# Softmax reciprocals of an attention layer's first two blocks computed in 16 columns, with three SyncE transfers to fold and spread them

## The reference, cut to what matters

```python
attn = jnp.einsum('bhdi,bhdj->bhij', q * scale, k)
attn = attn + pos[..., :, None] + pos[..., None, :]
attn = jax.nn.softmax(attn, axis=-1)
y = jnp.einsum('bhij,bhdj->bhdi', attn, v)
```

## Time and profile before

| | us |
|---|---|
| median of 3 runs | 514.74 (514.13 to 515.56) |
| profiled execution, its own time | 514.55 |
| its span in the profile | 512.8 |
| outside the span | 1.75 |
| mean granted TensorE clock | 0.98 |

### The profile page before, as it was taken

The page is one execution under the profiler, slowest core; times in us unless marked ns, Lnnn a source line. Parts: engine busy times, 40 slices in busy tenths (PEclk is TensorE's granted clock), DMA queues, the critical chain, the costliest instruction groups (busy, mean ns, idle before and its releaser), DMA issues.

```text
span 512.8 us, 7031 instructions
## 1 busy us (share of the span) xinstructions
PE 479.3 (93%) x2268; PEld 238.7 (47%) x2268; DVE 360.1 (70%) x687; ACT 273.3 (53%) x522; POOL 217.8 (42%) x203
## 2 busy tenths in 40 slices
PE   8799999999989899999999999999999989998996
PEld 6454444443237565444444322664544444432463
DVE  7599888976164568987887823738988787832573
ACT  3138776767514324876766762131777765764032
POOL 8300021001000002898879991000699888896000
PEclk9969999999998998999999999998999999999999
DMA  5330432000000054487944440034457854442002
GB/s 145 56 57 20 137 65 34 1 2 2 1 0 1 15 123 104 82 203 159 207 89 84 83 79 5 1 88 109 92 120 154 182 105 83 84 83 42 1 0 82
DMA packets 16419, 38.18 MB, mean 74 GB/s; under 512 B 4870, under 2 KB 6030, under 8 KB 16256
## 3 DMA queue, kind: packets, MB, share of 16 engines
q1 hardware_dynamic: 11088, 21.72, 17.7%
q0 software_dynamic: 5152, 16.00, 16.9%
q10 hardware_dynamic: 144, 0.02, 0.0%
HBM read 4.76 MB, written 1.05 MB: 11 GB/s over the span
## 4 chain that ended last, share of the span: by engine, by line
PE 68%; DVE 15%; DMA 4%; ACT 4%; issue 3%; SPq 3%; POOL 2%; ACTq 0%; POOLq 0%; DVEq 0%
PE PV L927 15%; PE S L889 15%; PE S L916 11%; DVE max L662 10%; PE S L1037 4%; DMA k_stack<-kL 4%; PE M L943 3%; PE PV L844 2%; PE S L870 2%; DVE rec_sb L692 2%; PE M L870 2%; PE PV L870 2%; PE S L907 2%; PE S L1082 2%; PE PV L863 1%
## 5 line engine op out<-in xcount | busy, mean ns | idle before, releaser
L662 DVE TENSOR_REDUCE max<-S 128x1 f32<-128x512 f32 x384 | 239.8, 669 | 20.8 <-PE S L889 20.6
L514 ACT ACTIVATE E<-S 128x512 f32<-128x512 f32 x384 | 212.6, 601 | 76.2 <-PE S L916 72.2
L450 POOL TENSOR_TENSOR SUMS<-E 128x512 f32<-128x512 f32 x126 | 167.0, 1476 | 123.9 <-ACT E L514 123.8
L889 PE MATMUL S<-k_stack,q_stack 126*128 126x512 f32 x384 | 183.2, 490 | 13.5 <-DVE max L662 8.7
L916 PE MATMUL S<-q_stack,k_stack 128*128 128x512 f32 x384 | 154.6, 411 | 2.7 <-ACT E L514 1.5
L889 PEld LDWEIGHTS S<-k_stack,q_stack 126*128 126x128 f32 x384 | 74.4, 194 | 92.9 <-DVE max L662 64.7
L927 PE MATMUL PV<-E,V 128*32 128x512 f32 x768 | 95.4, 599 | 1.7 <-ACT pv_sb L521 1.7
L916 PEld LDWEIGHTS S<-q_stack,k_stack 128*128 128x128 f32 x384 | 72.6, 191 | 33.3 <-ACT E L514 20.6
L692 DVE RECIPROCAL rec_sb<-den_sb 128x64 f32<-128x64 f32 (+1 forms) x54 | 35.7, 665 | 35.0 <-ACT den_sb L531 35.0
L503 ACT ACTIVATE mHL<-S 4x128 fp32r<-4x128 f32 x48 | 12.6, 263 | 55.2 <-PE S L907 55.2
L927 PEld LDWEIGHTS PV<-E,V 128*32 128x32 f32 x768 | 20.0, 109 | 45.2 <-issue 28.3
(11 more groups left out here) (180 smaller groups left out, 335.5 us busy)
## 6 DMA issues: line engine op xcount, KB each, us to landing
SUMS<-SUMS POOLq DMA_DIRECT2D x30, 512.0 KB, 5.1
k_stack<-kH SPq DMA_DIRECT2D x32, 128.0 KB, 3.0
q_stack<-qH SPq DMA_DIRECT2D x40, 64.0 KB, 2.0
k_stack<-kL SPq DMA_DIRECT2D x16, 128.0 KB, 3.2
q_stack<-qH SPq DMA_DIRECT2D x16, 128.0 KB, 2.3
q_stack<-mHL SPq DMA_DIRECT2D x96, 2.0 KB
q_stack<-qL SPq DMA_DIRECT2D x20, 64.0 KB, 2.0
X<-x_in_dram SPq DMA_DIRECT2D x2, 512.0 KB, 5.5
```

Of the source, the lines that this page charges most:

```text
L450: pool.tensor_tensor(SUMS[:, slot, :], E[:, E_PLAN[s][0], :], E[:, E_PLAN[s + 1][0], :], ALU.add).then_inc(sum_ready, 1)
L514: act.activation(E[:, slot, :], B[:, ring_of_scores(s) % B_RING, :], ACT.Exp, scale=1.0 if l == 0 else float(HEAD_DIM[l]) ** -0.5).then_in ...
L662: dve.tensor_reduce(max8[:, m % 2, r:r + 1], A[:, n % A_RING, :], AX.X, ALU.max, negate=True).then_inc(a_used, 1)
L889: pe.matmul(A[:, n % A_RING, :], q_stack[0:SHIFT_ROW, slot, q0:q0 + P], k_stack[0:SHIFT_ROW, slot, k0:k0 + HALF], start=True, stop=True).t ...
```

## The change

In each layer the reciprocals of blocks 0 and 1 are computed on four rows' worth of numbers instead of 128 rows, since the 32 rows of a head hold the same number. SP issues three transfers a block. `fold_sums` takes one row a head (four rows of 512) and lays it out as 128 partitions of 16 columns (`den_in`), 128 pieces of 64 bytes. DVE makes one reciprocal of 128x16 (`folded_reciprocals`, s = 66 and s = 98). `reciprocal_rows` writes the result back as rows 0, 32, 64, 96 of `den_sb`. `spread_reciprocals` copies each of these four rows to its head's 32 rows of `rec_sb`, 256 KB in pieces of 2 KB. On SP's list `fold_sums` of block 0 stands behind the last head's load (ahead of the weight load in layer 1), `reciprocal_rows` behind shift row 9, `spread_reciprocals` behind shift row 10; for block 1 the three stand behind shift rows 12, 13 and 14. POOL's `normalise` waits for the spread.

In layer 0 the fold reads `pv_sb`, and the gather matmul on PE and the copy to `den_sb` on ACT remain only for the later blocks. In layers 1 and 2 the fold reads `den_sb`, and ACT's copy moves from s = 59, 91, 123 to s = 54, 86, 118. The rest of the layer is as before. The diff, without the declarations of four semaphores and a removed constant:

```diff
@@ -42,8 +42,9 @@
...
-REC_PARTS = (8, 8, 2, 2)
-REC_STEP = 64
+FOLDED = 2
+REC_STEP = 66
+PER_ROW = HALF // DP
@@ -128,6 +129,8 @@
...
+        den_in = sb("den_in", [P, PER_ROW])
+        rec_out = sb("rec_out", [P, PER_ROW])
@@ -264,10 +267,15 @@
...
+        REC_L = 2 * (BLOCKS - FOLDED)
+        PV_OUTS = (4, 3, 3)
+        DEN_OUTS = (BLOCKS - 1 - FOLDED, BLOCKS - 1, BLOCKS - 1)
...
-            return REC_L * l + sum(REC_PARTS[:b + 1])
-
-        PV_OUTS, DEN_OUTS = (4, 3, 3), 3
+            return REC_L * l + 2 * (b - FOLDED + 1)
+        def den_count(l, b):
+            return sum(DEN_OUTS[:l]) + b + 1 - (0 if l else FOLDED)
@@ -320,6 +328,30 @@
...
                                  mHL[:, m % 2, r, :].bitcast(F32)).then_inc(shift_dma[m % 2], 16)
+            def fold_sums(l, b):
+                if l == 0:
+                    sp.wait_ge(pv_out, pv_count(l, b))
+                    src, row = pv_sb, DP // 2
+                else:
+                    sp.wait_ge(den_out, den_count(l, b))
+                    src, row = den_sb, 0
+                sp.dma_start(den_in[:, :], src[row:P:DP, :].rearrange("u (d n) -> u d n", n=PER_ROW)).then_inc(dens_folded, 16)
+            def reciprocal_rows(l, b):
+                sp.wait_ge(recs_folded, FOLDED * l + b + 1)
+                sp.dma_start(den_sb[0:P:DP, :].rearrange("u (d n) -> u d n", n=PER_ROW), rec_out[:, :]).then_inc(recs_rows, 16)
+            def spread_reciprocals(l, b):
+                sp.wait_ge(recs_rows, 16 * (FOLDED * l + b + 1))
+                sp.wait_ge(att_ready, (BLOCKS - 1) * l + b)
+                sp.wait_ge(att_tail, 2 * l)
+                sp.dma_start(rec_sb[:, :],
+                             den_sb[0:P:DP, :].rearrange("u (o n) -> u o n", o=1)
+                             .to_broadcast([HEADS_B, DP, HALF])).then_inc(recs_spread, 16)
@@ -360,11 +392,18 @@
...
                         shift_rows(l, h + 1)
+                fold_sums(l, 0)
                 if l == 1:
...
                     shift_rows(l, j)
+                    if j in (9, 13):
+                        reciprocal_rows(l, (j - 9) // HEADS_B)
+                    if j in (10, 14):
+                        spread_reciprocals(l, (j - 10) // HEADS_B)
+                    if j == 12:
+                        fold_sums(l, 1)
             for n in range(4):
@@ -421,7 +460,10 @@
...
                 g, f = b // 2, b % 2
-                pool.wait_ge(rec_ready, rec_count(l, b))
+                if b < FOLDED:
+                    pool.wait_ge(recs_spread, 16 * (FOLDED * l + b + 1))
+                else:
+                    pool.wait_ge(rec_ready, rec_count(l, b))
                 pool.tensor_tensor(att[:, g, HALF * f:HALF * (f + 1)], pv_sb[:, :], rec_sb[:, :],
@@ -523,11 +565,11 @@
...
                 if l == 0:
-                    act.wait_ge(gathered, b + 1)
+                    act.wait_ge(gathered, b - FOLDED + 1)
                 else:
                     act.wait_ge(den_done, DENS_L * (l - 1) + 2 * (b + 1))
-                if l + b:
-                    act.wait_ge(rec_ready, rec_count(l, b - 1) if b else REC_L * l)
+                act.wait_ge(recs_spread, 16 * (FOLDED * l + min(b, FOLDED)))
+                act.wait_ge(rec_ready, REC_L * l)
                 act.activation(den_sb[:, :], M[:, :], ACT.Copy).then_inc(den_out, 1)
@@ -564,9 +606,10 @@
...
                         numerators_out(l, (s - 57) // 32)
-                    den_step = 59 if l else 62
-                    if s >= den_step and (s - den_step) % 32 == 0:
-                        denominators_out(l, (s - den_step) // 32)
+                    den_step = 54 if l else 62
+                    b = (s - den_step) // 32
+                    if s >= den_step and (s - den_step) % 32 == 0 and (l or b >= FOLDED):
+                        denominators_out(l, b)
                 if l == 0:
@@ -675,20 +718,24 @@
...
+            def folded_reciprocals(l, b):
+                n = FOLDED * l + b
+                dve.wait_ge(dens_folded, 16 * (n + 1))
+                dve.wait_ge(recs_rows, 16 * n)
+                dve.reciprocal(rec_out[:, :], den_in[:, :]).then_inc(recs_folded, 1)
             def reciprocals(l, b, part):
-                wide = HALF // REC_PARTS[b]
-                cs = slice(wide * part, wide * (part + 1))
+                cs = slice(QUARTER * part, QUARTER * (part + 1))
                 if part == 0:
...
                     if b < BLOCKS - 1:
-                        dve.wait_ge(den_out, DEN_OUTS * l + b + 1)
+                        dve.wait_ge(den_out, den_count(l, b))
                     elif l == 0:
-                        dve.wait_ge(gathered, BLOCKS)
+                        dve.wait_ge(gathered, BLOCKS - FOLDED)
                     else:
                         dve.wait_ge(den_done, DENS_L * l)
-                    if b == 0 and l:
-                        dve.wait_ge(att_tail, 2 * l)
                 dve.reciprocal(rec_sb[:, cs], den_sb[:, cs] if b < BLOCKS - 1 else M[:, cs]).then_inc(rec_ready, 1)
@@ -697,7 +744,7 @@
...
-                    dve.wait_ge(rec_ready, REC_L * l + sum(REC_PARTS[:-1]) + part + 1)
+                    dve.wait_ge(rec_ready, rec_count(l, BLOCKS - 2) + part + 1)
@@ -738,11 +785,10 @@
...
                         split(l, LATE_DVE[l][s])
-                    b, part = (s - REC_STEP) // 32, (s - REC_STEP) % 32 // 2
-                    if 0 <= b < 2 and s % 2 == 0 and part < REC_PARTS[b]:
-                        reciprocals(l, b, part)
-                for part in range(REC_PARTS[2]):
-                    reciprocals(l, 2, part)
+                    if s >= REC_STEP and (s - REC_STEP) % 32 == 0 and (s - REC_STEP) // 32 < FOLDED:
+                        folded_reciprocals(l, (s - REC_STEP) // 32)
+                for part in range(2):
+                    reciprocals(l, BLOCKS - 2, part)
                 last_block(l)
@@ -932,7 +978,7 @@
...
                 if k == 0 and b:
-                    pe.wait_ge(den_out, DEN_OUTS * l + b)
+                    pe.wait_ge(den_out, den_count(l, b - 1))
                 first = HEADS_B * b
@@ -952,8 +998,8 @@
...
                 pe.wait_ge(pv_out, b + 1)
-                if b:
-                    pe.wait_ge(den_out, b)
+                if b > FOLDED:
+                    pe.wait_ge(den_out, b - FOLDED)
                 pe.matmul(M[:, :], gather[:, :], pv_sb[:, :], start=True, stop=True).then_inc(gathered, 1)
@@ -1008,8 +1054,8 @@
...
                             denominators(l, BLOCKS - 1, 0)
-                    if l == 0 and s >= 60 and (s - 60) % 32 == 0:
-                        gather_sums((s - 60) // 32)
+                    if l == 0 and s == 60 + 32 * FOLDED:
+                        gather_sums(FOLDED)
                 for t in range(5, TILES):
```

More of the change, by code:

```diff
@@ L195, in attention_chain @@
         rec_ready, att_ready, att_tail = sem("rec_ready"), sem("att_ready"), sem("att_tail")
+        dens_folded, recs_folded, recs_rows, recs_spread = (sem("dens_folded"), sem("recs_folded"), sem("recs_rows"),
+                                                            sem("recs_spread"))
         out_done, x_ready = sem("out_done"), sem("x_ready")
@@ L252, in sum_count @@
             return (l - 1) * SUMS_L + min(PAIRS * j + k + 1, SUMS_L)
-        REC_L = sum(REC_PARTS)
         RING_L = STEPS + UNITS_L
```

## The result

The changed kernel takes 510.87 us (median of 5 runs, 508.97 to 512.11) against 515.28 for the kernel before in the same comparison, a ratio of 0.9918 with a 95% interval from 0.9896 to 0.9941. Seven more runs gave a median of 510.49 us, ratio 0.9913 (0.9878 to 0.9949). The forecast was 508.5 in a range of 506.9 to 512.0: the direction and the range hold, but 4.4 us came where 6.2 were worked out.

The account below looks back on a forecast made before the run. Layer 0 was taken as bound by PE with DVE in the way, the ends of layers 1 and 2 by POOL and transfers. 514.55 - 4.07 - 2.2 = 508.3 us profiled, 508.5 for the median; range 506.9 to 512.0.

Parts of the forecast that it names:

- Layer 0: Two of three gather matmuls and the stalls of sixteen reciprocal parts go: 4.07 us summed over the layer's periods.
- base period: Undisturbed period between L927 groups in layer 1, 271.70 to 278.14: 6.44 us, against which longer periods were compared.
- last period with maxima: Layer 0, 115.69 to 122.01, only six maxima left: gain taken as 0.40 us, between 0 and 0.81.
- relief in layers 1 and 2: Shorter periods put PE 1.6 us ahead in a layer; 1.1 us a layer taken (0.8 to 1.6), 2.2 for both.
- period with the head's load: Layer 1, up to 256.49: PE stands for the load with or without reciprocals; gain 0, at most 0.4 us.
- 6.6 to 8 fits into 8.9: Block 1 of layer 1: the 256 KB spread takes 6.6 to 8 us, within 8.9 us before POOL wants it.
- rival A: Spread lands at about 10 us, holding POOL's normalise of block 1 by 1.1 us in layers 1 and 2: 510.5 us; chance 0.12.
- ScalarE's copy: Denominators' copy five steps earlier: at s = 118 it delays PE by one copy, within the 0.4 us PE can spare.
- The last 0.4 comes after that and is lost: End of layers 1 and 2: PE's last 0.4 us of gain comes after POOL's idle time and is lost to POOL.
- C: Fold lands late, 7.6 us instead of 5.59; DVE holds PE 2 us in layers 1 and 2: 512.3 us; chance 0.06.
- D: DVE isn't what lengthens the periods; only the two gather matmuls are won, 1.62 us: 512.9 us; chance 0.06.
- B: Spread takes 13 us, 4.1 late; layers 1 and 2 each lose 3.0 us: 516.5 us, slower; chance 0.06.

Follow-up runs that it names:

- both edits: Changed kernel with the spread's source rows in partitions 0, 36, 72, 108 and ScalarE's copy of the denominators back at s = 59, 91, 123: 507.62 us, ratio 0.9862.

## Why the prediction was right and where it was not

**Layer 0.** Each term came out: 4.07 predicted, 4.02 measured. The gathers were shown alone (1.6), the stalls alone (2.4), and they add. The base period from layer 1 was the right one for layer 0. The last period with maxima, taken by analogy at 0.40 between 0 and 0.81, was 0.41.

**The relief in layers 1 and 2.** 0.80, 0, 0.40 and 0.40 were predicted, and the groups in the first trace give 0.80, 0, 0.39 and 0.42. That the period with the head's load gives nothing was right in that trace; in the second it was 0.6 shorter (7.12 us), but it was also short, 7.26, with the reciprocals back, so this is not their relief.

**The spread.** The step that failed is "6.6 to 8 fits into 8.9". The window was 8.4 us (294.22, when POOL was ready, less 285.84), and the transfer took 9.6. Without the sums' folds the higher estimate, 6.6, was near the 7.1 measured; what was mis-sized is the term for the load beside it, 2.5 us and not up to 1.4. That the folds are this load is argued from layer 0, which has none; no run took them away. It isn't a fixed price either: from one port the same place added only 0.2 to 0.5 us (12.1 to 12.3 and 12.6). What followed is rival A, with its mechanism, its place and the length of its hold: 1.22 us in layer 1 and 0.89 in layer 2, where 1.1 were given. I had given it 0.12. That its 510.5 us lies near the profiled execution's 510.87 is in part luck: A had the whole gain of layers 1 and 2 gone, but they kept 1.0 us of it in that trace, and its hand-over was 1.0 longer. The second trace took 509.04.

**ScalarE's copy.** The prediction weighed it at s = 118 alone and there found it hidden. At s = 54 and 86, which it didn't look at, it cost 0.28 us each in both layers. This is the second term missing, about 1.1 us, shown by the run that puts it back. At s = 118 it was hidden only while the spread held POOL: with the rows 36 apart it lengthens the last period by 0.49 us in each of the two layers.

**The limit by POOL.** "The last 0.4 comes after that and is lost" used POOL's idle time as a cap. With both edits POOL followed further than that: layers 1 and 2 are 5.1 us shorter together than before (means of its two traces), where 2.2 were the forecast.

**The others.** The sign given for C, idle time of DVE before its 16 columns, was seen (0.56 us in layer 1), but it was too strict: the fold landed 3.6 us after its issue, not 7.6, and PE didn't wait, so C is excluded. D is excluded by layer 0. B was not met, but is real: the run with one port shows it at 12.1 us, in layers 1 and 2 with more than the price given, since PE's wait for the shift rows was not in it.

**What is left.** The profiled execution was forecast at 508.3 us and took 510.87. Of the 2.6 us between, the table puts 1.2 in layers 1 and 2 (1.0 gained for 2.2 forecast), 1.0 in the hand-over and 0.4 outside its stretches. On the means of two traces layers 1 and 2 gained 1.95 us, and that this is near 2.2 is luck: two errors of opposite sign. The relief that POOL could follow was 5.1 and not 2.2, by the run with both edits, and the held POOL (2.1) and the copies (1.1) took 3.2 back. With layer 0's 4.02 these 1.95 would make 6.0 us; the medians show 4.4. The lower granted clock in half of the runs fits about 1.1 of the difference (all twelve runs take 510.7 us on average, the six at the higher clock 509.6), and the prediction had no term for it. The lower end of its range, 506.9, is worked from 508.3; from the 508.5 of the medians it would be 507.1, which changes nothing here.

## What to carry to other kernels

Time periods of an unchanged instruction group with and without the suspected work; the difference, not the busy time, is what its removal brings: the sixteen reciprocals of layer 0, at 533 ns each, were 8.5 us of work and worth 2.4. When compute is replaced by transfers, give each new transfer the window between its issue and its first reader, in every layer, and time it under the load that runs beside it. And when one transfer reads few partitions, choose which: two small edits, of the source rows and of the place of a copy, took the gain from 0.8% to 1.4%. When a forecast comes out right, look whether its terms did: here two of them missed, in opposite directions.

## What the runs showed of the hardware

The time of the 256 KB spread depends on which partitions its four source rows stand in. From SP's issue to POOL's start in layer 0 it was 12.1 us with partitions 0 to 3, 7.1 with 0, 32, 64, 96, and 4.6 with 0, 36, 72, 108 as with 0, 4, 8, 12. That is about 2 us and 10 us divided by 1, 2 and 4, which is how many ports the Trainium skill (page "SBUF — State Buffer", section "Door 1: The DMA port swizzle") gives these rows; its 27.2 GB/s a port would make, as an estimate, 9.6, 4.8 and 2.4 us, and the measured steps of 5.0 and 2.5 agree. In layers 1 and 2, beside the sums' folds, the same transfer took 9.6 us instead of 7.1 with partitions 0, 32, 64, 96, but only 12.3 to 12.6 instead of 12.1 with partitions 0 to 3; why the load costs less there stays open.

A reciprocal of 128x16 took 233 ns, one of 128x64 533 ns.
